# A hybrid attention and state-space block: some products with C on GpSimd, and the causal corner zeroed there

## The reference

```
x = x + attention(layernorm(x))      # 16 heads of 16, rotary embedding, causal softmax
x = x + ffn(layernorm(x))            # rows quantised in blocks of 32, 256x256 product, bias
x = x + layernorm -> { u + mamba(rmsnorm(u)), then + silu(rmsnorm @ w1) @ w2 }
x = x + ffn(layernorm(x))
```

```
h_t = h_{t-1} * exp(dt_t * A) + (dt_t * u_t) * B_t     # 512 x 16 states
y_t = sum over the 16 states of h_t * C_t              # B_t, C_t: 16 numbers per time step
```

## Time and profile before

| what | before |
|---|---|
| median of 3 runs | 10632.09 us (10631.8 to 10632.46) |
| profiled execution | 10632.12 us |
| its span | 10630.5 us |
| PE busy | 8101.7 us, 76% |
| DVE busy | 8122.4 us, 76% |
| ACT busy | 4281.5 us, 40% |
| POOL busy | 3406.1 us, 32% |
| mean granted TensorE clock | 0.888 of full speed |

### The profile page before, as it was taken

How to read it: one execution, slowest core, us unless ns; L and a number is a source line. 1 busy time by engine, 2 the same in 40 slices (tenths; PEclk the granted TensorE clock), 3 DMA queues, 4 the chain that set the end, 5 groups by cost and what they waited for, 6 DMA issues and landing times. The chain is left out here.

```text
span 10630.5 us, 101592 instructions
## 1 busy us (share of the span) xinstructions
PE 8101.7 (76%) x34228; PEld 3995.5 (38%) x34228; DVE 8122.4 (76%) x12583; ACT 4281.5 (40%) x8183; POOL 3406.1 (32%) x1895
## 2 busy tenths in 40 slices
PE   5778787787867877777777778778777787777877
PEld 2343343433434334343343434334343243432434
DVE  5776968779687696877868778687786967869677
ACT  2424434254342533425335253342534435344342
POOL 0340614315043150422505225151240513406134
PEclk8898988889888898888989889898898988989889
DMA  3020020200202002030020300202011020200202
GB/s 72 1 43 6 4 45 0 48 1 8 41 0 48 1 11 38 0 48 1 17 33 0 49 1 20 29 0 49 1 29 21 0 49 1 36 13 4 45 0 48
DMA packets 249261, 230.18 MB, mean 22 GB/s; under 512 B 24006, under 2 KB 208582, under 8 KB 248534
## 3 DMA queue, kind: packets, MB, share of 16 engines
q1 hardware_dynamic: 248732, 223.49, 12.8%
HBM read 151.60 MB, written 70.25 MB: 21 GB/s over the span
## 5 line engine op out<-in xcount | busy, mean ns | idle before, releaser
L557 POOL TENSOR_TENSOR arena<-arena 128x1024 f32<-128x1024 f32 x1024 | 2409.3, 2354 | 2146.3 <-DVE arena L928 879.0
L696 ACT ACTIVATE PS<-arena,Aneg 128x512 f32<-128x512 f32 x2048 | 1413.6, 691 | 2046.5 <-DVE XNT L968 1079.9
L619 ACT ACTIVATE arena<-PS 128x512 f32<-128x512 f32 (+3 forms) x3072 | 1312.7, 501 | 957.6 <-PE PS L1135 800.7
L836 DVE TENSOR_REDUCE pm<-PS 128x1 f32<-128x512 f32 (+3 forms) x2048 | 1138.7, 584 | 577.4 <-PE PS L1111 396.8
L1230 PE MATMUL PS<-arena,sel 96*128 96x512 bf16 x2048 | 656.8, 404 | 1037.4 <-DVE arena L944 549.5
L1108 PE MATMUL PS<-arena 96*128 96x512 bf16 (+3 forms) x3072 | 1114.5, 380 | 370.6 <-PEq L1325 272.1
L511 POOL TENSOR_TENSOR rstd<-ve,mhalf 128x4 f32<-128x4 f32 x96 | 105.1, 1095 | 3168.6 <-DVE ve L734 3168.6
L1242 PE MATMUL PS<-arena,identf 128*128 128x512 f32 x2048 | 1070.6, 649 | 0.0
L1242 PE MATMUL PS<-XNT,identf 128*128 128x512 f32 x2048 | 970.8, 597 | 0.0
L1132 PE MATMUL PS<-arena 99*128 99x512 bf16 (+3 forms) x3072 | 924.3, 330 | 15.5 <-DMA arena<-arena 15.5
L1070 PE MATMUL PS<-identf,arena 128*128 128x128 f32 x1280 | 268.2, 369 | 778.5 <-POOL arena L527 663.4
(11 more groups left out here) (140 smaller groups left out, 13882.6 us busy)
## 6 DMA issues: line engine op xcount, KB each, us to landing
pieces_scratch<-arena SPq DMA_DIRECT2D x272, 192.0 KB, 2.5
arena<-pieces_scratch SPq DMA_DIRECT2D x102, 512.0 KB
arena<-pieces_scratch SPq DMA_DIRECT2D x204, 128.0 KB
arena<-pieces_scratch SPq DMA_DIRECT2D x102, 256.0 KB
arena<-in_x SPq DMA_DIRECT2D x17, 1024.0 KB, 5.6
U<-in_x SPq DMA_DIRECT2D x17, 1024.0 KB, 5.5
out<-X SPq DMA_DIRECT2D x64, 256.0 KB, 18.0
arena<-arena SPq DMA_DIRECT2D x192, 8.0 KB, 1.9
```

Source lines behind the costliest of these rows:

```text
L557: nc.gpsimd.tensor_tensor(DB[:, n % 2], DTU[:, j, half(th)].unsqueeze(1).to_broadcast([P, SP2, TH]), BB[:, SP2 * sg:SP2 * (sg + 1), :], AL ...
L619: A(PT[:, (s % 2) * HG + hh, 0:w], bank(t_bank(n))[:, 0:w], ACT.Exp, scale=DH ** -0.5)\
L696: A(bank(da_bank(m)), DT[:, j, half(th)], ACT.Exp, scale=Aneg[:, j, SP2 * sg + ss:SP2 * sg + ss + 1]).then_inc(S("dA"), 1)
L836: V_.tensor_reduce(out=dst, in_=bank(u % 3)[:, 0:w], op=ALU.max, axis=AX.X, negate=True).then_inc(S("red"), 1)
```

## The change

Scan: of the eight units of a block, units 2 and 6 (four of sixteen states) are multiplied by C on POOL, from a copy of the spread C in SBUF (CB). PE spreads C for these units only in the first block of each half, and ACT then copies the two banks to CB. On POOL the product of unit n-2 follows the DB of unit n. POOL's addition of DT and DTU stands ahead of unit 2 instead of unit 3. The wait for DVE's products becomes a wait for POOL's where the unit is POOL's.

Attention: `mask2` and its matmul go. After the exponentials of a step with a diagonal, POOL zeroes the corner above the diagonal, four blocks of 128 by 128, in place. PV stands one step later (`s + 2`), waits for the corner, and PT has three buffers.

```diff
-        PT = view(20480, 4096).rearrange("p (s t) -> p s t", s=2 * HG)
+        PT = [view(at, 2048).rearrange("p (s t) -> p s t", s=HG) for at in (20480, 22528, 29696)]
+        CB = view(24592, 2 * SP2 * TH).rearrange("p (g s t) -> p g s t", g=2, s=SP2)
-        pv_at = [STEP_AT + HG * (s + 1) for s in range(NST * NG)]
+        pv_at = [STEP_AT + HG * (s + 2) for s in range(NST * NG)]
+        DIAG_STEP = [q0 == j * P for _, _, _, _, j, q0, _ in (t_unit(HG * s) for s in range(NST * NG))]
+        POOL_SG = (2, 6)
+        # pool_c(n): unit n's sg is in POOL_SG; kept_c: also j == 0; spread_c: kept_c or not pool_c
...
@@ pool_program
+            for s in range(NST * NG):
+                if DIAG_STEP[s]:
+                    corner = PT[s % len(PT)][:, :, 0:P]
+                    pool.wait_ge(S("expd"), HG * (s + 1))
+                    nc.gpsimd.affine_select(out=corner, in_=corner, pattern=[[0, HG], [1, P]],
+                                            compare_op=ALU.is_ge, fill=0.0, base=0, channel_multiplier=-1)\
+                      .then_inc(S("cut"), 1)
...
+            def times_kept_c(k):
+                _, kth, _, ksg = m_unit(k)
+                hs = HS[k % len(HS)]
+                pool.wait_ge(S("h"), SP2 * (k + 1))
+                if kth < NTH - 1:
+                    pool.wait_ge(S("hl"), k + 1)
+                pool.wait_ge(S("Ce"), before(kept_c, k + 1))
+                nc.gpsimd.tensor_tensor(hs, hs, CB[:, POOL_SG.index(ksg)], ALU.mult).then_inc(S("hP"), 1)
-                if sg == 3 and jt + 1 < NJT:
+                if sg == 2 and jt + 1 < NJT:
...
+                if n >= 2 and pool_c(n - 2):
+                    times_kept_c(n - 2)
+            times_kept_c(NM - 2)
@@ scalar_program
+                if n >= 1 and kept_c(n - 1):
+                    _, _, _, ksg = m_unit(n - 1)
+                    act.wait_ge(S("Cg"), before(spread_c, n))
+                    if before(pool_c, n - 1):
+                        act.wait_ge(S("hP"), before(pool_c, n - 1))
+                    A(CB[:, POOL_SG.index(ksg)], PS[:, c_bank(0):c_bank(0) + SP2, :], ACT.Copy).then_inc(S("Ce"), 1)
@@ vector_program
-                if n >= 1:
+                if n >= 1 and dve_c(n - 1):
                     times_c(n - 1)
@@ tensor_program, attention
-                    if diag:
-                        ins = MM(bank(t_bank(n))[:, 0:P], identb[:, :], mask2[:, :], start=False, stop=True)
...
+                    if DIAG_STEP[s]:
+                        pe.wait_ge(S("cut"), sum(DIAG_STEP[:s + 1]))
@@ tensor_program, scan
-                    if n >= 1:
-                        pe.wait_ge(S("hC"), n)
-                    for ss in range(SP2):
+                    if spread_c(n):
+                        if before(dve_c, n):
+                            pe.wait_ge(S("hC"), before(dve_c, n))
+                        if before(kept_c, n):
+                            pe.wait_ge(S("Ce"), before(kept_c, n))
+                        for ss in range(SP2):
...
-                    pe.wait_ge(S("hC"), k + 1)
+                    if pool_c(k):
+                        pe.wait_ge(S("hP"), before(pool_c, k + 1))
+                    else:
+                        pe.wait_ge(S("hC"), before(dve_c, k + 1))
```

More of the change, by code:

```diff
@@ L96, in build @@
         mask1 = sb("mask1", [P, P], BF16)
-        mask2 = sb("mask2", [P, P], BF16)
         cosT = sb("cosT", [P, NT, DH])
@@ L284, in _ @@
                 nc.vector.tensor_copy(mask1[:, :], mst[:, 0, :])
-                nc.vector.tensor_copy(mask2[:, :], mst[:, 1, :])
                 nc.vector.tensor_copy(sel[:, :, :], stage[0:3 * 2 * DS])
@@ L374, in c_bank, with pool_c, kept_c, spread_c @@
             return ss
+        POOL_SG = (2, 6)
+        def pool_c(n):
+            return m_unit(n)[3] in POOL_SG
+        def kept_c(n):
+            return pool_c(n) and m_unit(n)[2] == 0
+        def spread_c(n):
+            return kept_c(n) or not pool_c(n)
+        def before(which, n):
+            return sum(which(k) for k in range(n))
+        def dve_c(n):
+            return not pool_c(n)
         def z_bank(k):
@@ L616, in scalar_program @@
                     act.wait_ge(S("ST"), n + 1)
-                    if s >= 2:
-                        act.wait_ge(S("PV"), s - 1)
-                    A(PT[:, (s % 2) * HG + hh, 0:w], bank(t_bank(n))[:, 0:w], ACT.Exp, scale=DH ** -0.5)\
+                    if s >= len(PT):
+                        act.wait_ge(S("PV"), s - len(PT) + 1)
+                    A(PT[s % len(PT)][:, hh, 0:w], bank(t_bank(n))[:, 0:w], ACT.Exp, scale=DH ** -0.5)\
                         .then_inc(S("expd"), 1)
@@ L942, in times_c @@
                     dve.wait_ge(S("hl"), n + 1)
-                dve.wait_ge(S("Cg"), n + 1)
+                dve.wait_ge(S("Cg"), before(spread_c, n + 1))
                 V_.tensor_tensor(hs, hs, PS[:, c_bank(0):c_bank(0) + SP2, :], ALU.mult)\
@@ L1130, in tensor_program @@
                         pe.wait_ge(S("expd"), n - 2 if n < T6 else n - 5)
-                    diag = q0 == j * P
-                    ins = MM(bank(t_bank(n))[:, 0:w], KS[0:SR + PIECES, h, tile(j)],
-                             QS[0:SR + PIECES, h, q0:q0 + w], start=True, stop=not diag)
-                    if diag:
-                        ins = MM(bank(t_bank(n))[:, 0:P], identb[:, :], mask2[:, :], start=False, stop=True)
-                    ins.then_inc(S("ST"), 1)
+                    MM(bank(t_bank(n))[:, 0:w], KS[0:SR + PIECES, h, tile(j)],
+                       QS[0:SR + PIECES, h, q0:q0 + w], start=True, stop=True).then_inc(S("ST"), 1)
                 if u >= pv_at[0] and (u - pv_at[0]) % HG == 0 and (u - pv_at[0]) // HG < NST * NG:
@@ L1145, in tensor_program @@
                         ins = MM(PS[VW * hh:VW * (hh + 1), 6, TH - w:TH], V[:, j, g * HG + hh, :],
-                                 PT[:, (s % 2) * HG + hh, 0:w], start=j == 0, stop=s == last_of[oc])
+                                 PT[s % len(PT)][:, hh, 0:w], start=j == 0, stop=s == last_of[oc])
                     ins.then_inc(S("PV"), 1)
@@ L1226, in tensor_program @@
                         spread_b(ahead[1] * NSG + ahead[3])
-                    if n >= 1:
-                        pe.wait_ge(S("hC"), n)
-                    for ss in range(SP2):
-                        ins = MM(bank(c_bank(ss)), sel[:, DS + SP2 * sg + ss, :], BCP[:, half(th)],
-                                 start=True, stop=True)
-                    ins.then_inc(S("Cg"), 1)
+                    if spread_c(n):
[4 more added lines that the diff above has]
+                        for ss in range(SP2):
+                            ins = MM(bank(c_bank(ss)), sel[:, DS + SP2 * sg + ss, :], BCP[:, half(th)],
+                                     start=True, stop=True)
+                        ins.then_inc(S("Cg"), 1)
                 if n >= 1:
```

## The result

After: 10459.44 us, the median of four runs (10456.77 to 10460.25), against 10631.94 (10629.89 to 10632.46) for the kernel before beside it. The ratio is 0.9838 [0.9821, 0.9855]. 172 us less is 10.8 a pass; the forecast was 208 us and 13.0 a pass. The profiled execution took 10459.04, span 10457.4.

A forecast was written before the change was run, and what follows sets the result against it. PE was taken to pace attention and DVE the scan. Scan 8.5 plus attention 4.5 (4.9 + 1.1 - 1.2 - 0.3) gave 13.0 us per pass, 208 over 16 passes: 10632 to 10424 us, range 10336 to 10520, chance 0.60.

The forecast's parts named there:

- What bounds each stage: Whole pass: PE sets the pace of attention (busy 86.9 of 87 us in one stretch), DVE that of the scan.
- A product moved: Scan: a product with C takes 2.31 us to the next start on POOL and frees 1.11 us on DVE.
- The steady block: Scan, eight units in the first half: 29.36 us falls to 27.78, saving 1.6, with 0.57 turned into waits for POOL.
- the layout: Scan: hand-drawn schedule of POOL and DVE through one steady block, ending at 27.78 us, with a 0.41 us wait.
- times_u: Scan, a DVE instruction in each block: stays at 1.94 us beside a running DB on POOL, against 0.68 alone.
- The first blocks and the entry into the second half: Scan, first block of each half: ACT's copies of C and POOL's products lose 1.25 us per block.
- The masks: Attention: removing 128 mask matmuls a pass from PE gives 4.9 + 1.1 us.
- the 88 from the 40: Attention: 88 masks where PE is full, 0.056 us each, 4.9 us; 40 in the last 35 us, half counted, 1.1.
- The cut: Attention: POOL's zeroing of the corner takes 0.9 us, covered except at the pass's end, where it costs 1.2 us.
- PV later, and the third buffer: Attention: PV one step later covers the cut, the third PT buffer keeps exponentials in place; PE's added waits cost 0.3 us.
- Rival A: Scan: POOL limits it; at 2.5 us a product 8.5 us shrinks to 1.2, at 2.7 it loses 11; chance 0.13.
- The rule weighed: Attention: two-input DVE and POOL instructions exclude each other; some 4 us of DVE per pass, within its 15 us slack.

The follow-up runs named there:

- att_only: Kernel after with every product with C back on DVE, so only the attention part of the change: 10577.67 us, ratio 0.9956.
- scan_only: Kernel after with attention as before (mask matmul, two PT buffers, earlier PV, no cut), so only the scan part: 10507.44 us, ratio 0.9891.
- b_early: Kernel after plus three DB buffers, DVE's own products in each half's first block, second half's B spread and copied two units earlier: 10274.25 us, ratio 0.9664.
- db3: Kernel after with three DB buffers instead of two, so POOL may run one unit further ahead: 10406.51 us, ratio 0.9799.
- first_dve: Kernel after with the products of the first block of each half back on DVE: 10414.29 us, ratio 0.9799.
- keep_mask: Kernel after with the 128 mask matmuls per pass left on PE as well as the cut on POOL: 10533.09 us, one run.
- no_cut: Kernel after without the corner's zeroing on POOL and PE's wait for it, so it computes something else: 10422.69 us, one run.

## Why the prediction was right, and what was off

The total fell by 172 us where 208 was forecast. The scan gave 23 us less than forecast (16 x 1.41), attention 8 us more (16 x 0.53), and 21 us were lost in stages for which nothing had been forecast.

**What bounds each stage** held: of attention and scan, att_only and scan_only move just the one that each touches.

**A product moved** held to its price, 2349 ns against 2.35. **The steady block** held to 0.01 us, with its wait in the place and of the size of the layout. One block of the first half was the steady one: block 1 took 28.08, and block 3 took 28.79 and not 27.78, since the entry into the second half already costs it 1.0 us (b_early). **Its times_u** held too, and I read too little in it: I priced it at 1.94 because it starts under DB7, and took that as given. It hung on POOL never being ahead (db3).

**The first blocks and the entry into the second half** are the term that was mis-sized. I put 2 x -1.25 + 3 x 1.6 = +2.3 us on the first five blocks; by the table of blocks they gave -2.21 + 1.27 + 1.55 + 0.55 - 0.90 = +0.26. The three others gave 1.54 + 2.26 + 3.10 = 6.90 against 6.15. Together 7.16 against 8.45. The step that was off is "POOL idled about 1 us per unit; the remaining 1.3 us of each product reaches the next scans". By first_dve the two products of block 0 came back as 5.4 us of waiting, 2.7 each, so POOL's idle time gave no cover, and something was added to the product's own 2.35. What was added stands in the timeline of that block: ys waits 2.83 us for the product and then takes 3.41 us, at a mean granted clock of 0.56, where it takes 1.98 in the steady block, and the spread of B stands behind it. How the 5.4 us split between POOL's time, the queue and the clock is not shown for this block, since b_early moves the spreads of the second half alone. The copies of C, for which the term held a part, cost nothing that shows (first_dve). Of PE's wait for the product I had named what is queued behind it, the next spread, and then looked only at whether ys itself had room. B's spread in the same queue did not: 1.0 us of block 3 and 4.5 of block 4 came back in b_early, though 1.7 were lost in block 6.

**The masks**: 4.53 of 6.0 (keep_mask). The experiment doesn't split the 88 from the 40, so whether the one or the other was priced too high stays open. **The cut**: 0.635 us, inside its bounds and near the one-input row of 0.62; I took 0.9. The estimate from the Trainium skill (GPSIMD Engine Reference, 4.1 Engine selection), 0.5 us, was 0.14 too low, my figure 0.27 too high. Its cost at the end of the pass was priced at 1.2; all cuts of a pass cost attention 0.40 (no_cut), and 0.49 of the 0.79 us by which the stretch at the end grew is the cut's. **PV later, and the third buffer**, priced at -0.3 for PE's waits, gained instead: attention in keep_mask has the masks and the cut and is still 0.50 below before, so without the 0.40 of the cut these two would give 0.90. That is what is left over, an estimate; no run has these two alone. In sum 4.53 - 0.40 + 0.90 = 5.03. Three terms were off by 1.5, 0.8 and 1.2 us and nearly cancelled; the good total of attention is partly luck.

**Rival A's prices** (1.2 us left of the scan at 2.5 us a product, 11 us a pass lost at 2.7) came without a layout. By my own sum POOL would have 10 x 2.5 + 1.22 = 26.2 us of work in a block of 27.8 at 2.5, so they are not shown, and no run tested them.

**The rule weighed** cost attention nothing that shows: the folds of the maxima take 174 to 176 ns in all 64 records of the kernel after and 174 to 177 before, and no_cut, without any cut beside the maxima, has 0.40 us less, of which PE's waits at the end are 0.3. It was decisive for db3, in the scan, where I had not weighed it. The Trainium skill (SBUF — State Buffer, Who interferes with whom) says that the two exclude each other for a whole instruction. The traces agree: in every kernel of this study each times_u that starts beside a POOL instruction ends 0.54 to 0.57 us behind the end of that instruction's record, whether it lasts 0.70 or 2.38 us, and each that starts with POOL idle takes 0.68 to 0.70.

**What wasn't forecast**: 1.16 us a pass in MLP and front, 3 us at the start and 2 at the end. The change edits no line there, but for one mask that is no longer built at the start. The runs say that the part in MLP and front comes with the cut: 150.03 in att_only against 148.25 in scan_only, 150.01 in keep_mask, which has the cut, against 148.62 in no_cut, which has not. The three kernels without the cut lie at 148.25 to 148.92, the ten with it at 149.46 to 151.16, one profiled execution of each. The time lies in the wait for the output at the end of a pass: from DVE's last addition to the next first maximum, in which PE, DVE and ACT have next to nothing to do, it is 18.53 us before, 20.99 after, 19.21 in scan_only and 19.56 in no_cut, while the rest of the stage is 130.39, 129.09, 129.04 and 129.06. The queue's own waits, before and after (in total, times, longest):
```profile
SPq L485 <- DMA out<-X: 237.3, 16, 15.6
```
```profile
SPq L507 <- DMA out<-X: 271.6, 16, 18.7
```
That is 14.8 and 17.0 us a pass. Time at the level 0.5 (1.2 GHz of 2.4) goes with the length of the stage: 43.8 us a pass before, 44.5 after, 43.1 in no_cut and 42.8 in scan_only. But what was added from before to after lies in that idle stretch (13.3 and 17.2 us), so it follows the wait and doesn't cause it. Why the output lands later where POOL cuts is open; no run was made on that. It moves totals by some 20 us, so for small edits I compare stages, not totals, and the cut's price is more than the 0.40 us of its own stage.

Also open: db3 and first_dve take 3.3 and 3.2 us off the scan and both together 8.5, more than the sum. The blocks say where (block 1, and block 6: 30.04 and 29.47 alone, 28.36 together, 30.05 again in b_early), not why.

## What to carry to other kernels

When work moves to an emptier engine, its price there is the smaller question. Ask which in-order queue will now wait for the new producer and what is behind that wait, and follow it until it comes back to the producer: here one move of a spread by two units was worth 45 us, with no work taken away. Look at the granted clock behind such a wait too: where it was near 0.5, the wait cost more than its own length. Give the helper engine one buffer more than it needs: it takes away waits, and where two engines can't run a kind of instruction at once, it also lets the helper be idle when the other comes.

## What the hardware showed

A cut of 4 x 128 x 128 elements in place costs 635 ns on POOL, in all 512 records together, and the last one of a pass starts 0.06 us behind its exponentials (9954.52 after 9954.46). POOL's product with two f32 inputs stays within 1% (means of 2349 to 2359 ns) in every kernel of this study, while DVE's two-input times_u beside it varies from 0.68 to 2.38 us: it ends 0.55 us behind the POOL instruction that it met.

In the kernel after the projections take one of two lengths, 111.2 to 111.4 us or 114.2 to 114.6, with the same instructions. Windows of two passes:
```profile
298.41:412.97 114.56, 79.55 (x212) 43.46 (x212) 81.84 (x165) 47.73 (x73) 19.16 (x15) 0.78 0.00 0
...
2878.13:2989.41 111.28, 74.86 (x212) 40.74 (x212) 81.70 (x164) 47.61 (x73) 19.16 (x15) 0.80 0.00 0
```
Same counts on PE, and 4.7 us more of its busy time in the longer one at a lower mean clock (0.78 against 0.80).
